# GpSimd's weight splits moved early and paused, routing moved ahead, and a new order of the last sums, in a one-core attention and mixture-of-experts kernel

## The reference, cut to what matters

```python
logits = xf @ Wr + br                       # 8 experts
topv, _ = lax.top_k(logits, 2)
masked = jnp.where(logits >= topv[:, 1:2], logits, -jnp.inf)
weights = jax.nn.softmax(masked, axis=-1)   # the routes
h = gelu(einsum('td,edh->eth', xf, W1) + b1)          # 128 -> 512
expert_out = einsum('eth,ehd->etd', h, W2) + b2       # 512 -> 128
out = einsum('etd,te->td', expert_out, weights)
x = x + tanh(g_ffn) * out
```

## Time and profile before

| what | us |
|---|---|
| median of 3 runs (lowest, highest) | 133.28 (131.89, 133.32) |
| the profiled execution, whole | 132.46 |
| its span in the trace | 130.2 |
| outside the span (132.46 - 130.2) | 2.3 |

### The profile page before, as it was taken

One profiled execution on the slowest core, in us unless ns is written; L12 is line 12 of the kernel. 1 busy time (PEld: TensorE's weight loads), 2 busy tenths in 40 slices (PEclk: granted clock), 3 DMA queues, 4 the chain that ended last, 5 costly groups with the idle time before them and its releaser, 6 DMA issues.

```text
span 130.2 us, 1685 instructions
## 1 busy us (share of the span) xinstructions
PE 117.5 (90%) x575; PEld 94.7 (73%) x575; DVE 89.9 (69%) x175; ACT 80.5 (62%) x107; POOL 62.9 (48%) x50
## 2 busy tenths in 40 slices
PE   6999969998878993959999999999999999999950
PEld 2397555544465891939999999999999999999930
DVE  1583687529386498999679877775775775775991
ACT  3027764401355755928878878878878878878900
POOL 0001460005203999999999999980330330330802
PEclk9999995559999999999999999999999999999998
DMA  3896000000310215400891340030040030000003
GB/s 93 234 406 249 0 0 5 3 0 0 101 60 0 82 79 161 162 6 9 238 337 43 107 146 0 0 141 0 0 141 3 5 141 0 0 0 0 0 0 141
DMA packets 3833, 10.07 MB, mean 77 GB/s; under 512 B 697, under 2 KB 1066, under 8 KB 3826
## 3 DMA queue, kind: packets, MB, share of 16 engines
q1 hardware_dynamic: 3154, 9.43, 21.5%
q10 hardware_dynamic: 672, 0.55, 1.5%
HBM read 9.49 MB, written 0.49 MB: 77 GB/s over the span
## 4 chain that ended last, share of the span: by engine, by line
PE 70%; DVE 14%; ACT 5%; issue 5%; POOL 2%; POOLq 1%; DVEq 0%
PE bank L772 23%; PE bank L799 22%; PE bank L641 7%; PE bank L658 3%; ACT prod L409 3%; POOL cf L329 2%; DVE hidl L617 2%; PE bank L664 2%; ACT hidh L416 2%; DVE prod L496 2%; DVE tw L496 2%; PE bank L718 2%; PE bank L735 1%; DVE qk L261 1%; PE bank L748 1%
## 5 line engine op out<-in xcount | busy, mean ns | idle before, releaser
L617 DVE TENSOR_TENSOR hidl<-prod,hidh 128x896 fp32r<-128x896 f32 (+1 forms) x34 | 45.3, 1339 | 19.8 <-ACT hidh L416 19.8
L409 ACT ACTIVATE prod<-bank,col_sb 128x896 f32<-128x896 f32 (+1 forms) x34 | 32.9, 967 | 14.5 <-PE bank L772 11.8
L323 POOL TENSOR_TENSOR wel<-we_sb,weh 128x512 fp32r<-128x512 f32 x16 | 25.6, 1604 | 20.9 <-issue 19.9
L416 ACT CAST hidh<-prod 128x896 fp32r<-128x896 f32 (+1 forms) x34 | 30.5, 899 | 1.0
L329 POOL TENSOR_TENSOR cf<-cf,kf 128x448 f32<-128x448 f32 x12 | 17.9, 1496 | 26.6 <-DVE kf L604 26.4
L799 PE MATMUL bank<-hidl,weh 128*128 128x448 f32 x64 | 18.5, 368 | 2.2 <-DVE hidl L617 2.2
L772 PE MATMUL bank<-xth,weh 128*128 128x448 f32 x64 | 18.6, 366 | 0.3 <-ACT xth L404 0.3
L772 PE MATMUL bank<-xtl,weh 128*128 128x448 f32 x64 | 18.6, 367 | 0.0
L772 PE MATMUL bank<-xth,wel 128*128 128x448 f32 x64 | 18.5, 365 | 0.0
L799 PE MATMUL bank<-hidh,weh 128*128 128x448 f32 x64 | 18.4, 367 | 0.0
L799 PE MATMUL bank<-hidh,wel 128*128 128x448 f32 x64 | 18.3, 365 | 0.0
(11 more groups left out here) (118 smaller groups left out, 116.7 us busy)
## 6 DMA issues: line engine op xcount, KB each, us to landing
we_sb<-in_w_experts SPq DMA_DIRECT2D x8, 512.0 KB, 5.0
route_b<-route_scratch SPq DMA_DIRECT2D x8, 448.0 KB, 3.6
out<-vf SPq DMA_DIRECT2D x2, 224.0 KB, 1.9
tb<-in_tab_b SPq DMA_DIRECT2D x1, 297.0 KB, 6.3
ta_c<-in_tab_ctx SPq DMA_DIRECT2D x1, 274.8 KB, 4.9
wa_sb<-in_w_attn SPq DMA_DIRECT2D x1, 256.0 KB, 5.7
x_sb<-in_x SPq DMA_DIRECT2D x1, 224.0 KB, 3.8
x_sb<-in_x ACTq DMA_DIRECT2D x1, 224.0 KB, 4.1
```

Of the source, the lines that this page charges most:

```text
L323: gp.tensor_tensor(wel[:, e, k, :], we_sb[:, e % RING, k, :], weh[:, e, k, :].bitcast(F32), ALU.subtract).then_inc(we_split, 1)
L409: act.activation(hid[:, n % 2, halves, :], bank[:, 2 * (n % 2):2 * (n % 2) + 2, 0:TOK][:, halves, :], ACT.Gelu, bias=col_sb[:, P_B1 + n:P_ ...
L416: act.copy(hidh[:, n % SLOTS, halves, :], hid[:, n % 2, halves, :]).then_inc(hid_hi, 1)
L617: ve.tensor_tensor(hidl[:, n % SLOTS, halves, :], hid[:, n % 2, halves, :], hidh[:, n % SLOTS, halves, :].bitcast(F32), ALU.subtract).then ...
```

## The change

Four things are done.

- GpSimd makes the rests for experts 0 and 1 as soon as VectorE has copied the turned shift weights (L538, `wt_ok`), one behind the other. Before, expert 0 waited for the first output spectrum and expert 1 for the normalised x. Then GpSimd waits for the finished routes (`route_ok`) before expert 2.
- `logit_differences()` goes ahead of hidl(0), the tanh ahead of step 1's gelu on ScalarE. The first four operations of `routes()` become `chosen()`, behind hidl(1); the other four stay behind hidl(2).
- At the end VectorE takes both halves of expert 7 before it makes a sum. GpSimd now helps with the first half's sum (208 of its 448 columns), where before it made 160 columns of the second half's.
- SyncE's program is the same but for the place of one wait: the store of the first half of the output waits for GpSimd's part.

```diff
@@ sync
-                if half == 1:
+                if half == 0:
                     sp.wait_ge(sum_p, 1)
@@ gpsimd
                 if e == 0:
-                    gp.wait_ge(of_ok[0], 1)
-                if e == 1:
-                    gp.wait_ge(xn_v, sum(by_vector))
+                    gp.wait_ge(wt_ok, 2)
+                if e == LEAD_BY_SCALAR:
+                    gp.wait_ge(route_ok, 1)
...
-            gp.wait_ge(scaled_ok, 2 * E)
+            gp.wait_ge(scaled_ok, 2 * (E - 1) + 1)
             gp.wait_ge(acc_ok, 2 * (E - 2))
-            gp.tensor_tensor(o_sb[:, 1, CUT:], acc[:, 1, CUT:], scaled[:, 1, CUT:], ALU.add).then_inc(sum_p, 1)
+            gp.tensor_tensor(o_sb[:, 0, 0:CUT], acc[:, 0, 0:CUT], scaled[:, 0, 0:CUT], ALU.add).then_inc(sum_p, 1)
@@ scalar
-                if n == 1:
+                if n == 0:
                     act.wait_ge(ldif_ok, 1)
                     act.activation(ltanh[:, :, :], ldif[:, :, :], ACT.Tanh, scale=0.5).then_inc(ltanh_ok, 1)
@@ vector
+            logit_differences()
             for n in range(E * HC):
...
-                if n == 0:
-                    logit_differences()
+                if n == 1:
+                    chosen()
                 if n == 2:
                     routes()
...
             for half in range(2):
                 take_expert(E - 1, half)
-                end = TOK if half == 0 else CUT
+            ve.wait_ge(acc_ok, 2 * (E - 2))
+            for half in range(2):
+                first = CUT if half == 0 else 0
                 ve.wait_ge(scaled_ok, 2 * (E - 1) + half + 1)
-                ve.wait_ge(acc_ok, 2 * (E - 2))
-                ve.tensor_tensor(o_sb[:, half, 0:end], acc[:, half, 0:end], scaled[:, half, 0:end], ALU.add).then_inc(sum_v, 1)
+                ve.tensor_tensor(o_sb[:, half, first:], acc[:, half, first:], scaled[:, half, first:], ALU.add).then_inc(sum_v, 1)
```

More of the change, by code:

```diff
@@ L236, in tiled @@
             return t.rearrange("p (i d) -> p i d", d=D)
-        CUT = 288
+        CUT = 208
         def norm_counts(n, times):
@@ L576, in logit_differences, with chosen @@
                 mark(ve.tensor_tensor(lmask[:, :, :], logit[:, :, :], ltop[:, :, 1:2].broadcast_to([PT, NT, E]), ALU.is_ge))
-            def routes():
+            def chosen():
                 ve.wait_ge(ltanh_ok, 1)
@@ L583, in routes @@
                 link(ve.reciprocal(lrec[:, :, :], lden[:, :, :]))
-                link(ve.tensor_tensor(lexp[:, :, :], lnum[:, :, :], lrec[:, :, :], ALU.mult))
+                mark(ve.tensor_tensor(lexp[:, :, :], lnum[:, :, :], lrec[:, :, :], ALU.mult))
+            def routes():
+                settle()
                 link(ve.tensor_tensor(lexp[:, :, :], lexp[:, :, :], lmask[:, :, :], ALU.mult))
```

## The result

The changed kernel takes 138.24 us in the median of 4 runs (136.54 to 138.93), the kernel before 132.82 in the same comparison (4 runs). The ratio is 1.037, with a 95% interval of 1.025 to 1.050: it is slower. The profiled execution took 137.98 us, its span is 136.1.

The account below looks back on a forecast made before the run. TensorE was taken as the bound, its idle stretches coming from VectorE's routing chain. The profiled 132.46 us plus 2.3 for the later project(8), plus 2.2 for the clock, minus 0.3 for the last sums gave 136.7, range 132.8 to 139.0.

Parts of the forecast that it names:

- The routing: VectorE's routing ahead of the first rests: routes at 51.5 us, 4.1 us won if nothing else were late.
- Four pairs: GpSimd's four pairs from 51.5, beside hidl(3) to hidl(7), take 11.2 us, so expert 3 is split at 62.7.
- The store behind the load: In SyncE's queue the routes' store, issued at 63.1, lands behind expert 6's 512 KB load, at 66.5.
- The take to project(8): On VectorE take(0, 0), hidl(8) and take(0, 1) take 2.6 us with gaps; project(8) may start at 72.9.
- The clock: TensorE's clock falls to 1.2 GHz behind the longer idle time, costing 2.2 us, between 0 and 5.
- The last sums: At the end, both takes first let the second half's sum of 448 columns start earlier: 0.3 us won.
- The sums: GpSimd's first sum, behind all twelve pairs, comes at 83.6 to 84 for take(2, 0) at 83.4: cost 0, up to 1.1.
- experts 0 and 1 during the weight spectra: 0.2 us won: Ahead of the loop, GpSimd's four early rests take some 5.8 us; the routes then come at 51.5.
- What VectorE does meanwhile reads PSUM: Reason given that VectorE isn't slowed beside the early rests: takes last 0.67 or 0.68 beside busy or quiet GpSimd.
- the sums decide: Rival, chance 0.08: routes come early enough but GpSimd's first sum, at 85, holds up hidl(14); 133.3 us.
- GpSimd's quiet as what makes the routing fast: Ahead of hidl(0), quiet GpSimd lets VectorE's logit operations take 1.6 us in all, ending at 44.8 at no cost.
- 2 us for all that follows: If the logit operations ahead of hidl(0) stayed slow, they and all that follows would come some 2 us later.

Follow-up runs that it names:

- the fillers: The changed kernel with 30 filler matmuls in TensorE's idle stretch ahead of project(8): 135.79 us, ratio 1.019 to the kernel before.
- the experiment with the store first: The changed kernel with the routes' store and the first three route_b loads ahead of expert 6's load in SyncE's queue: 135.61 us, ratio 1.020.
- the pause ahead of expert 3: The changed kernel with GpSimd's pause ahead of expert 3, not 2, and expert 6's load behind the routes in SyncE's queue: 133.56 us, against 133.74 before.
- the routing alone: The kernel before with only logit_differences(), the tanh and chosen() moved as in the change, without a pause: 129.33 us, ratio 0.970.
- The second run of the pause at 4: The changed kernel with the pause ahead of expert 4, not 2, run again beside the kernel with an earlier start: 130.0 us, ratio 0.957 to before.

## Why the prediction was right, and where it was off

**The direction, the place and the mechanism were right.** The store left at 65.6, not when `route_t` was ready; take(0, 0) waited for it; TensorE stood idle for 7.06 us ahead of project(8), and the clock fell behind that. Three experiments show each as a cause: with the store ahead of load 6 the stretch gets shorter (2.72 us), with the fillers it loses its low clock, and with the pause ahead of expert 4 it is gone.

**Term by term**, forecast and measured in the profile after:
- The routing: the routes 9.6 us behind the loop's start (forecast 51.5 against 42.0, so 9.5). The logit operations took 1.55 us (forecast 1.6). Right.
- Four pairs: 12.0, forecast 11.2. The second alone took 3.9, beside hidl(4) and hidl(5) in a row.
- The store behind the load: 2.97, forecast 3.4. From the issue of the first `route_b` to the take: 4.3, forecast 3.8.
- The take to project(8): 2.4, forecast 2.6. TensorE's idle stretch ahead of it: 7.06, forecast 6.6.
- The clock: 1.5 to 1.7, forecast 2.2.
- The last sums: 0.3, as forecast.
- The sums: nothing, as forecast. The first ended at 86.0, the take was at 88.1.
- Together: project(8) started 4.7 us later than before (75.26 against 70.57), forecast 2.3. Of the 2.4 between them, 1.5 are the front.

**What was mis-sized is the front.** The step "experts 0 and 1 during the weight spectra: 0.2 us won" measured 1.3 us lost until the loop starts. Part of its reason failed: "What VectorE does meanwhile reads PSUM" did not hold, as the clock was high in that stretch of this execution, the work came earlier, and the first `of` product fell beside the rests (1.69 us for 0.64). But this is not what moved the start. VectorE began its normalised x at 38.10, against 39.29 before, so up to there the changed kernel was 1.2 us ahead. What came late was TensorE. In this execution the clock was low twice ahead of the loop, the second time from 37 to 44 us, and the filler matmuls that stand there ahead of the turned x took 3.19 us, from 38.81 to 42.00, in the earlier trace rows 1.74, to 41.04; before it was low once, from 19.7 to 29.9. The turning behind them took 1.70 for 0.93. When and for how long it is low differs from profile to profile (last section), and the start of the loop with it. The prediction read one execution's front as if it were fixed.

The clock's term rests in part on a reading that the rows don't bear out. The prediction took the 13 fillers at the start of the program, 0.41 us each, as a low stretch of 5 us. The granted clock reads 1.00 there, from 0 to 8 us, so the profile doesn't say why these fillers were slow. The low stretch that the rows do show, 10 us, would have given 5.1; the one behind the idle time held for 6.7 us, of which 3.2 fell on matmuls, from 75.26 on.

**On the rivals.** The sums as a second limit were given as "the sums decide": the experiment with the store first shows it behind the first limit, at 4.97 us of wait, and the pause ahead of expert 3 shows it alone, at 4.31. The prediction took GpSimd's quiet as what makes the routing fast. That was right for the operations and wrong for the time: the routing alone wins its 3.2 us beside a busy GpSimd. I had priced that case as 2 us for all that follows.

The Trainium skill, page DMA: Bandwidth & Descriptors, section Queues, rings and completion order, was drawn on in the prediction. The traces agree with it: the store behind a load took 2.97 us, without it 1.71.

## What to carry to other kernels

Before an engine is made to pause, list what is queued behind its results, not only on it, and put transfers that are waited for ahead of those that are merely early: here a load that waited for the paused engine stood ahead of the store that everyone waited for, and a wait of 8.8 us became a stop of 7 us for TensorE. Keep a busy neighbour away from chains of tiny operations on the critical path (7.1 us for 2.2), but not from those that lie in a gap. And when a change has several parts, run the parts alone: the routing was worth 3% by itself, and the same pause two experts later turned 4% slower into 5% faster.

## What the runs showed of the hardware

- Operations on 8 columns of VectorE took 0.17 us beside a quiet GpSimd. Beside its pairs they took 0.52 (a cast) or 0.85 to 1.12 us (a subtraction), and each of these ended 0.02 or 0.03 us behind the operation of GpSimd that was running, in the kernel without a pause and in both profiles of the pause at 4; those that started just ahead of GpSimd's next took 0.17. So here a tiny operation costs what is left of the large one beside it. The takes, which read PSUM, took 0.67 to 0.69 us in all 14 profiles.
- Six matmuls of the loop took 1.22 us in eight profiled executions and 1.24 in six (365 and 368 ns for one), all at a granted clock of 1.00, with no wait between them. I don't know why.
- In each of the 14 profiles TensorE's granted clock was 1.2 GHz for some time ahead of the loop or around its start, in one piece or two: 3.4 us in the second profile of the pause at 4, where the loop starts at 40.4; 6.8 in four kernels, with starts from 41.2 to 41.9; 10.2 in before, after and two more, with starts from 42.2 to 43.5; 13.7 in three, with starts from 43.4 to 44.9. The two profiles of the pause at 4, one kernel, had 6.8 and 3.4. Two kernels stand apart: the one that starts expert 0's rests at once had 10.2 and starts at 44.3; the one without a pause, which starts at 49.2, had 3.4 from 20 on and 10.2 from 44.3 to 54.5. The second run of the pause at 4 has spans from 124.9 us, at a mean granted clock of 0.984, to 130.7 at 0.935. So the spread of the times goes with the clock; where in those executions it was low isn't on record, and no experiment set it.
